# Attention kernel: second passes of the 512-wide look-ahead and score blocks as 64-row matmuls issued in a row

## The chip, the cores and the metric

The kernel runs on one core of one Trainium2 chip. The metric is the device time of one execution in microseconds. TensorE (PE) does the matmuls, ScalarE (ACT) and VectorE (DVE) read its results out of PSUM, GpSimd (POOL) masks and normalizes, and SyncE (SP) issues the DMAs.

## The reference

For each of 8 batches of 512 tokens by 256, with 8 heads of 64:

```python
xn = layernorm(x)
qu, ku, vu, qc, kc, vc = split(xn @ W_qkv.T)            # 6 x 8 heads x 64
term1 = where(causal_mask, 0.0, (qc * SCALE) @ vu.T)
lookahead = where(causal_mask, sigmoid((qu * SCALE) @ ku.T), 0.0)
Su = einsum('bhij,bhkj->bhik', term1, lookahead)
scores = (qc * SCALE) @ kc.T - silu(Su)
attn = softmax(where(causal_mask, neg, scores))
out = (attn @ vc) @ W_out.T
y = x + out + (silu(xn @ wg.T) * (xn @ wu.T)) @ wd.T
```

## The kernel before

Three stages run one after the other: a prologue that transposes `W_qkv` (to about 18 us), `attention` over all batches (to about 1000 us), and `ffn_and_sum`. The change touches `attention` alone.

Every fp32 value is kept as a high and a low part in a rounded 32-bit format, and a product is a sum of passes over them (`PRODUCTS`: high-high, high-low, low-high). Heads are 64 wide and the array has 128 rows. For the look-ahead and the scores the two halves of the rows are used: for head `h`, the 64 partitions with the head's index hold the high part of `ku` (or `kc`), the other 64 the low part; `qu_s` and `qc_s` hold for index `HIGH` the high part of q in both halves, and for `LOW` the low part in both. The first matmul of a block (`a = HIGH`) therefore sums high-high and low-high at once, the second (`a = LOW`) adds q's low part times both halves of k.

**Steps.** The stage runs 64 steps, one head each (`g = b * HEADS + s`), written out for s = 0 to 7 in a loop over batches (`FIRST` for batch 0, `MIDDLE` for 1 to 6, `LAST` for 7). Work on a head is spread over three steps: in step g the look-ahead and `term1` blocks of head g, the scores of head g - 1 (`back1`), the turning of probabilities and the product with v of head g - 2 (`back2`). Even steps also project QC, V and KC of the next pair of heads, odd steps QU, KU and VU. The order of each engine's instructions is written out by hand in `even_step` and `odd_step` of each engine, and engines are held together by counting semaphores alone; an engine's queue is in order.

**Blocks.** The causal triangle of 512 by 512 is in three groups j: j = 0 is the row block of width 512, j = 1 those of 384 and 128, j = 2 that of 256. `look_ahead(j)` (L681) is two matmuls a row block into a bank of X; ScalarE takes tanh of it (`tanh_of_L`, L875). `scores(j)` does the same products (L709) into `Sc`, then, at j = 0 after waiting for all of T and L of its head, the matmuls of `Su` (L719, twelve for j = 0) into another bank; ScalarE's `gate_of` (L899) reads `Su`, VectorE's `silu_of` (L1111) and `minus_scores` (L1122) follow.

**X banks.** Four PSUM banks are handed round in the order in which PE fills them (`X_ORDER`). A block's `into_x` waits until the block that had the bank four fills earlier has been read. For `("L", s, 0)` of an even step s = 2, 4, 6 that is the head product `("O", s - 1, 0)`, free when `sum_o` (L1154, VectorE) of the odd step is done. (In batch 0, s = 2, it is a `T` block.) For s = 0 of batches 1 to 7 it is the KU projection of step 7, and `("L", 0, 1)` has the bank of VU. In an even step `look_ahead(0)` also waits for KU's low part and for the doubled `qu_s`:

```python
if s % 2 == 0 and j == 0:
    pe.wait_ge(qu_twice, (b * PAIRS + s // 2 + 1) * 32)
    bank, filled = into_x(part, b, ("L", s, j), proj_low, lambda b: proj_count(b * PAIRS + s // 2, KU))
```

**Around the change.** PE ends an odd step with `project(KU)`, `project(VU)` (L638, six 512-wide matmuls each) and begins the even step with `scores(g - 1, s1, 0)`, then `look_ahead(0)`, `look_ahead(1)`, and the transposes of probabilities (L733). ScalarE ends the odd step with `high_proj(KU)` (L855, two copies of 64 partitions), `copy_o_low` (L921), `exp_of(2)`, `high_proj(VU)`; VectorE with `low_proj(KU)` (L1052, two), `inverse(2)`, `sum_o`, `low_proj(VU)` (L1052).

Of the kernel before, what the change touches and what calls it, by code (L numbers as in the profile page):

```python
# [11 lines left out]
P = 128  # L12
# [279 lines left out]
def attention(nc, x, w_gate, w_up, w_down, W_out, sh, heads_out):  # L292
# [4 lines left out]
    with ctx:  # L297
# [101 lines left out]
        def proj_count(q, t):  # L399

            if isinstance(q, int) and q == 0:
                return FIRST_PAIR.index(t) + 1
            return q * 5 + PROJ_ORDER.index(t) + 1
# [201 lines left out]
        def _(pe):  # L605
# [64 lines left out]
            def look_ahead(part, b, s, j):  # L670

                if s % 2 == 0 and j == 0:
                    pe.wait_ge(qu_twice, (b * PAIRS + s // 2 + 1) * 32)
                    bank, filled = into_x(part, b, ("L", s, j), proj_low,
                                          lambda b: proj_count(b * PAIRS + s // 2, KU))
                else:
                    bank, filled = into_x(part, b, ("L", s, j))
                for w in ROWS[j]:
                    J, at = w - 1, WIDE[w] - GROUP[j][0]
                    for a in (HIGH, LOW):  # L680
                        last = pe.matmul(bank[:, at:at + w * P], ku_s[:, s % 2, J * P:(J + 1) * P],  # L681
                                         qu_s[:, s % 2, a, 0:w * P], start=(a == 0), stop=(a == 1))
                last.then_inc(filled, 1)

            def term1(part, b, s, j):

                par = (s // 2) % 2
                if s % 2 == 0 and j == 0:
                    pe.wait_ge(qc_twice, (b * PAIRS + s // 2 + 1) * 32)
                    bank, filled = into_x(part, b, ("T", s, j), proj_low,  # L690
                                          lambda b: proj_count(b * PAIRS + s // 2, VU))
                else:
                    bank, filled = into_x(part, b, ("T", s, j))
                for w in ROWS[j]:
                    J, at = TT - w, WIDE[w] - GROUP[j][0]
                    for a in (HIGH, LOW):
                        last = pe.matmul(bank[:, at:at + w * P], vu_s[:, s % 2, J * P:(J + 1) * P],  # L697
                                         qc_s[:, par, s % 2, a, J * P:SEQ], start=(a == 0), stop=(a == 1))
                last.then_inc(filled, 1)

            def scores(g, s, j):

                hp, par, slot = s % 2, (s // 2) % 2, (s + j) % 2
                if not (isinstance(g, int) and 3 * g + j < 2):
                    pe.wait_ge(scores_emptied, 3 * g + j - 1)
                for w in ROWS[j]:
                    I, at = w - 1, WIDE[w] - GROUP[j][0]
                    for a in (HIGH, LOW):
                        pe.matmul(Sc[slot][:, at:at + w * P], qc_s[:, par, hp, a, I * P:(I + 1) * P],  # L709
                                  kc_s[:, par, hp, 0:w * P], start=(a == 0), stop=(a == 1))  # L710
                if j == 0:
                    pe.wait_ge(T_ready, after(g, 3, 2))
                    pe.wait_ge(L_ready, after(g, 3, 2))
                for w in ROWS[j]:
                    I, at = w - 1, WIDE[w] - GROUP[j][0]
                    for J in range(I, -1, -1):
                        to = WIDE[TT - J] + (I - J) * P
                        for n, (a, c) in enumerate(PRODUCTS):
                            last = pe.matmul(Su[slot][:, at:at + (J + 1) * P], T_s[:, hp, a, to:to + P],  # L719
                                             L_s[:, hp, c, WIDE[J + 1]:WIDE[J + 1] + (J + 1) * P],  # L720
                                             start=(J == I and n == 0), stop=(J == 0 and n == 2))
                last.then_inc(scores_filled, 1)
# [29 lines left out]

            def even_step(part, b, s, g, s1, back1, back2, ahead):
                if back1:
                    scores(g - 1, s1, 0)
                look_ahead(part, b, s, 0)
                look_ahead(part, b, s, 1)
                if back2:
                    turn_probs(part, b, s, g - 2, 0)
                    turn_probs(part, b, s, g - 2, 1)  # L760
                    turn_probs(part, b, s, g - 2, 2)
                look_ahead(part, b, s, 2)
                if back1:
                    scores(g - 1, s1, 1)
                term1(part, b, s, 0)
                if s == 6:
                    transpose_x(part, b, s, b + 1)
                if back2:
                    attend(part, b, s, g - 2)
                if back1:  # L770
                    scores(g - 1, s1, 2)
                term1(part, b, s, 1)
                term1(part, b, s, 2)
                if ahead:
                    if s == 6:
                        pe.wait_ge(xT_low, (b + 1) * KD)
                    project(part, b, s, QC, (s // 2 + 1) % PAIRS)
                    values(part, b, s)
                    project(part, b, s, KC, (s // 2 + 1) % PAIRS)
                if part == LAST:  # L780
                    turn_weights(part, b, s, WEIGHTS_IN_STEP.get(s, ()))

            def odd_step(part, b, s, g, s1, back1, back2, ahead):
                look_ahead(part, b, s, 0)
                if back1:
                    scores(g - 1, s1, 0)
                look_ahead(part, b, s, 1)
                if back2:
                    turn_probs(part, b, s, g - 2, 0)
                look_ahead(part, b, s, 2)  # L790
                if ahead:
                    project(part, b, s, QU, (s // 2 + 1) % PAIRS)
                if back2:
                    turn_probs(part, b, s, g - 2, 1)
                if back1:
                    scores(g - 1, s1, 1)
                term1(part, b, s, 0)
                if back2:
                    turn_probs(part, b, s, g - 2, 2)
                term1(part, b, s, 1)  # L800
                if back1:
                    scores(g - 1, s1, 2)
                if back2:
                    attend(part, b, s, g - 2)
                term1(part, b, s, 2)
                if ahead:
                    project(part, b, s, KU, (s // 2 + 1) % PAIRS)
                    project(part, b, s, VU, (s // 2 + 1) % PAIRS)
                if part == LAST:
                    turn_weights(part, b, s, WEIGHTS_IN_STEP.get(s, ()))  # L810
# [27 lines left out]
        def _(act):  # L838
# [83 lines left out]

            def even_step(part, b, s, g, s1, back1, back2, ahead):
                par = (s // 2 + 1) % 2
                if back1:
                    gate_of(g - 1, s1, 0)
                tanh_of_L(part, b, s, g, 0)
                tanh_of_L(part, b, s, g, 1)
                if back2:
                    high_PT(part, b, s, g - 2, 0)  # L930
                    high_PT(part, b, s, g - 2, 1)
                tanh_of_L(part, b, s, g, 2)
                if back2:
                    high_PT(part, b, s, g - 2, 2)
                high_L(g, s, 0)
                if back1:
                    gate_of(g - 1, s1, 1)
                high_T(part, b, s, g, 0)
                if s == 6:
                    high_xT(part, b, s)  # L940
                if back1:
                    exp_of(g - 1, s1, 0)
                if back2:
                    copy_o_low(part, b, s, g - 2)
                high_L(g, s, 1)
                if back1:
                    gate_of(g - 1, s1, 2)
                high_T(part, b, s, g, 1)
                high_T(part, b, s, g, 2)
                if back1:  # L950
                    exp_of(g - 1, s1, 1)
                high_L(g, s, 2)
                if ahead:
                    high_proj(part, b, s, QC, par)
                    high_values(part, b, s)
                if back1:
                    exp_of(g - 1, s1, 2)
                if ahead:
                    high_proj(part, b, s, KC, par)
                if part == LAST:  # L960
                    high_weights(part, b, s, WEIGHTS_IN_STEP.get(s, ()))
# [669 lines left out]
```

## Time and profile before

| | us |
|---|---|
| median of 2 runs | 1201.75 (1200.53 to 1202.97) |
| span of the profiled execution | 1197.5 |
| PE busy | 1155.7 |
| DVE busy | 1046.0 |
| ACT busy | 924.4 |
| POOL busy | 543.8 |

The span runs from the first to the last instruction of the profiled execution. Matmuls overlap each other, so a PE that shows as busy is not thereby at its peak: how fast blocks follow one another is read from their starts in the timeline.

### The profile page before, as it was taken

How to read it: one execution, taken by the hardware profiler on the slowest of the kernel's cores; microseconds unless marked ns; L12 is line 12 of the kernel's file. 1: busy time of each engine (PE TensorE's matmuls, PEld its weight loads, DVE VectorE, ACT ScalarE, POOL GpSimd, SP SyncE). 2: the span in 40 equal slices, each digit the busy share in tenths (PEclk: the TensorE clock that was granted, in tenths of full speed). 3: DMA queues.
4: the chain of work that ended last, by engine and by line, in shares of the span. 5: the costliest groups of instructions: out<-in, count | busy, mean ns of one | idle time of the engine just before them, and what ended most of it. 6: DMA issues, size and time to landing. Idle time of an engine off the chain costs nothing. (4 is left out here: it accounts for less than half of the span.)

```text
span 1197.5 us, 25023 instructions
## 1 busy us (share of the span) xinstructions
PE 1155.7 (97%) x7324; PEld 1049.7 (88%) x7324; DVE 1046.0 (87%) x2421; ACT 924.4 (77%) x2074; POOL 543.8 (45%) x915
## 2 busy tenths in 40 slices
PE   6999999999999999999999999999999987999997
PEld 5899898989898989898989898989899976999997
DVE  6799889989998999899989998999889987878885
ACT  5788888888888888888888888888888864434443
POOL 0455555546555555555655565556555550000000
PEclk9999999999999999999999999999999998999999
DMA  5111211121112111211121112111321112243332
GB/s 172 40 45 45 63 45 45 45 63 44 44 44 63 44 44 44 63 44 44 44 63 44 44 44 63 44 44 44 101 59 45 45 54 79 89 140 102 108 109 67
DMA packets 41491, 74.16 MB, mean 62 GB/s; under 512 B 3504, under 2 KB 24496, under 8 KB 41392
## 3 DMA queue, kind: packets, MB, share of 16 engines
q1 hardware_dynamic: 41392, 73.15, 21.2%
q14 instruction: 75, 0.61, 0.2%
q8 instruction: 24, 0.39, 0.1%
HBM read 27.00 MB, written 12.58 MB: 33 GB/s over the span
## 5 line engine op out<-in xcount | busy, mean ns | idle before, releaser
L719 PE MATMUL Su<-L_s,T_s 128*128 128x128 f32 (+3 forms) x1920 | 292.5, 299 | 1.8 <-POOL T_s L543 1.8
L719 PEld LDWEIGHTS Su<-L_s,T_s 128*128 128x128 f32 x1920 | 279.3, 190 | 16.4 <-POOL T_s L543 2.7
L553 POOL TENSOR_SCALAR prob<-prob,inv 128x512 f32<-128x512 f32 x252 | 274.5, 1096 | 13.1 <-DVE inv L1134 12.9
L638 PE MATMUL X<-xT,W 128*128 128x512 f32 x960 | 242.5, 394 | 3.0 <-PEq L130 3.0
L638 PEld LDWEIGHTS X<-xT,W 128*128 128x128 f32 x960 | 172.7, 189 | 33.6 <-issue 3.2
L527 POOL TENSOR_SCALAR_AFFINE_SELECT gate<-gate 128x128 f32<-128x128 f32 (+1 forms) x192 | 66.3, 346 | 262.3 <-DVE gate L1111 197.3
L899 ACT ACTIVATE gate<-Su 128x512 f32<-128x512 f32 (+1 forms) x192 | 101.4, 528 | 71.5 <-PE Su L719 70.4
L907 ACT ACTIVATE prob<-prob,least 128x512 f32<-128x512 f32 (+3 forms) x256 | 142.4, 561 | 7.6 <-DVE least L1122 7.2
L1111 DVE SCALAR_TENSOR_TENSOR gate<-gate,Su 128x512 f32<-128x512 f32 (+1 forms) x192 | 114.2, 595 | 27.3 <-ACT gate L899 17.4
L543 POOL TENSOR_SCALAR_AFFINE_SELECT T_s<-T_s 128x256 fp32r<-128x256 f32 x256 | 131.1, 542 | 13.3 <-DVE T_s L1103 9.2
L535 POOL TENSOR_SCALAR_AFFINE_SELECT tanh_l<-tanh_l 128x128 f32<-128x128 f32 (+1 forms) x192 | 62.6, 333 | 160.0 <-ACT tanh_l L875 157.8
L681 PE MATMUL X<-qu_s,ku_s 128*128 128x512 f32 (+3 forms) x512 | 115.2, 335 | 11.4 <-DVE vu_s L1052 6.1
L882 ACT ACTIVATE T_s<-X 128x512 fp32r<-128x512 f32 (+1 forms) x192 | 97.4, 527 | 36.7 <-PE X L697 36.7
L1141 DVE TENSOR_TENSOR PT_s<-X,PT_s 128x512 fp32r<-128x512 f32 (+1 forms) x192 | 108.8, 594 | 19.1 <-ACT PT_s L915 18.1
L1122 DVE CUSTOM_DVE_ANT_0 prob<-Sc,gate 128x512 f32<-128x512 f32 (+3 forms) x256 | 117.8, 478 | 7.5 <-issue 6.2
L1095 DVE SCALAR_TENSOR_TENSOR L_s<-tanh_l,L_s 128x512 fp32r<-128x512 f32 (+1 forms) x192 | 121.1, 631 | 1.5 <-ACT L_s L890 1.5
L697 PE MATMUL X<-qc_s,vu_s 128*128 128x512 f32 (+3 forms) x512 | 115.2, 339 | 3.3 <-DVE qu_s L1052 2.1
L1103 DVE TENSOR_TENSOR T_s<-X,T_s 128x512 fp32r<-128x512 f32 (+1 forms) x192 | 113.5, 592 | 3.7 <-ACT T_s L882 1.1
L709 PE MATMUL Sc<-kc_s,qc_s 128*128 128x512 f32 (+3 forms) x512 | 115.6, 327 | 0.2 <-DVE least L1122 0.2
L875 ACT ACTIVATE tanh_l<-X 128x512 f32<-128x512 f32 (+1 forms) x192 | 99.5, 529 | 11.5 <-PE X L681 10.5
L890 ACT ACTIVATE L_s<-tanh_l 128x512 fp32r<-128x512 f32 (+1 forms) x192 | 104.7, 564 | 2.0 <-POOL tanh_l L535 1.6
L681 PEld LDWEIGHTS X<-qu_s,ku_s 128*128 128x128 f32 x512 | 84.0, 189 | 22.8 <-DVE vu_s L1052 9.0
(85 smaller groups left out, 2132.7 us busy)
## 6 DMA issues: line engine op xcount, KB each, us to landing
qu_s<-qu_s SPq DMA_DIRECT2D x64, 256.0 KB, 3.7
qc_s<-qc_s SPq DMA_DIRECT2D x64, 256.0 KB, 3.5
xb<-in_L_attn_x SPq DMA_DIRECT2D x16, 512.0 KB, 4.6
heads_out<-o_s SPq DMA_DIRECT2D x32, 256.0 KB, 2.0
f_o_in<-heads_out SPq DMA_DIRECT2D x8, 1024.0 KB, 5.7
f_xres<-in_L_attn_x SPq DMA_DIRECT2D x8, 512.0 KB, 4.6
out<-f_y SPq DMA_DIRECT2D x8, 512.0 KB, 3.2
w_raw<-in_L_attn_W_qkv SPq DMA_DIRECT2D x6, 512.0 KB, 7.4
```

The source lines that it names most:

```text
L543: last = pool.affine_select(out=v, in_=v.bitcast(F32), compare_op=ALU.is_ge, fill=0.0, base=0, pattern=[[0, 2], [1, P]], channel_multiplie ...
L553: last = pool.tensor_scalar(v, v, inv[:, hp, w - 1:w], None, ALU.mult)
L638: last = pe.matmul(bank[:, :], sh.W[:, a, k, cols], xT[:, c, k, :], start=(n == 0), stop=(n == 3 * KD - 1))
L681: last = pe.matmul(bank[:, at:at + w * P], ku_s[:, s % 2, J * P:(J + 1) * P], qu_s[:, s % 2, a, 0:w * P], start=(a == 0), stop=(a == 1))
L697: last = pe.matmul(bank[:, at:at + w * P], vu_s[:, s % 2, J * P:(J + 1) * P], qc_s[:, par, s % 2, a, J * P:SEQ], start=(a == 0), stop=(a = ...
L709: pe.matmul(Sc[slot][:, at:at + w * P], qc_s[:, par, hp, a, I * P:(I + 1) * P], kc_s[:, par, hp, 0:w * P], start=(a == 0), stop=(a == 1))
L719: last = pe.matmul(Su[slot][:, at:at + (J + 1) * P], T_s[:, hp, a, to:to + P], L_s[:, hp, c, WIDE[J + 1]:WIDE[J + 1] + (J + 1) * P], start ...
L907: last = act.activation(v, v, ACT.Exp, bias=least[:, hp, w - 1:w], scale=-1.0, accum_out=total[:, hp, w - 1:w])
L1095: dve.scalar_tensor_tensor(L_s[:, s % 2, LOW, c:c + n], tanh_l[:, c:c + n], 1.0, L_s[:, s % 2, HIGH, c:c + n].bitcast(F32), ALU.add, ALU.s ...
L1103: dve.tensor_tensor(T_s[:, s % 2, LOW, c:c + n], bank[:, 0:n], T_s[:, s % 2, HIGH, c:c + n].bitcast(F32), ALU.subtract) \
L1111: dve.scalar_tensor_tensor(gate[:, c:c + n], gate[:, c:c + n], 1.0, Su[(s + j) % 2][:, 0:n], ALU.add, ALU.mult).then_inc(silu_done, 1)
L1122: last = dve.tensor_tensor_reduce(prob[:, hp, WIDE[w]:WIDE[w] + w * P], Sc[(s + j) % 2][:, at:at + w * P], gate[:, WIDE[w]:WIDE[w] + w * P ...
```

## The change

A new function `first_products` issues four 512-wide matmuls: the high pass of `look_ahead(0)`, the high pass of the Sc product of `scores(g - 1, s1, 0)`, and then the two second passes, each over 64 rows (the partitions that hold the high part of `ku` or `kc`; q's low part times k's low part is left out of them). As the two heads are of different parity, the two second passes lie on different halves of the array, and they go into different banks. `scores` gets an argument that leaves the products out. It is called in all 32 odd steps and in the 31 even steps with `back1`, so 63 times; in the odd steps the look-ahead was already ahead of the scores, in the even steps this order is new. In the even steps ScalarE takes `tanh_of_L(0)` ahead of `gate_of(0)`. The narrower row blocks (384, 128, 256) stay as they are, and so do the other engines and the DMAs.

```diff
--- before.py
+++ after.py
@@ -682,6 +682,27 @@
                                          qu_s[:, s % 2, a, 0:w * P], start=(a == 0), stop=(a == 1))
                 last.then_inc(filled, 1)
 
+            def first_products(part, b, s, g):
+
+                if s % 2 == 0:
+                    pe.wait_ge(qu_twice, (b * PAIRS + s // 2 + 1) * 32)
+                    bank, filled = into_x(part, b, ("L", s, 0), proj_low,
+                                          lambda b: proj_count(b * PAIRS + s // 2, KU))
+                else:
+                    bank, filled = into_x(part, b, ("L", s, 0))
+                back = g - 1
+                hp, par, slot = (s - 1) % 2, ((s - 1) % HEADS // 2) % 2, (s - 1) % 2
+                pe.matmul(bank[:, :], ku_s[:, s % 2, (TT - 1) * P:SEQ], qu_s[:, s % 2, HIGH, :], start=True, stop=False)
+                if not (isinstance(back, int) and back == 0):
+                    pe.wait_ge(scores_emptied, 3 * back - 1)
+                pe.matmul(Sc[slot][:, :], qc_s[:, par, hp, HIGH, (TT - 1) * P:SEQ], kc_s[:, par, hp, :],
+                          start=True, stop=False)
+                mine, other = slice((s % 2) * DH, (s % 2 + 1) * DH), slice(hp * DH, (hp + 1) * DH)
+                pe.matmul(bank[:, :], ku_s[mine, s % 2, (TT - 1) * P:SEQ], qu_s[mine, s % 2, LOW, :],
+                          start=False, stop=True).then_inc(filled, 1)
+                pe.matmul(Sc[slot][:, :], qc_s[other, par, hp, LOW, (TT - 1) * P:SEQ], kc_s[other, par, hp, :],
+                          start=False, stop=True)
+
             def term1(part, b, s, j):
 
                 par = (s // 2) % 2
@@ -698,12 +719,12 @@
                                          qc_s[:, par, s % 2, a, J * P:SEQ], start=(a == 0), stop=(a == 1))
                 last.then_inc(filled, 1)
 
-            def scores(g, s, j):
+            def scores(g, s, j, products_done=False):
 
                 hp, par, slot = s % 2, (s // 2) % 2, (s + j) % 2
-                if not (isinstance(g, int) and 3 * g + j < 2):
+                if not products_done and not (isinstance(g, int) and 3 * g + j < 2):
                     pe.wait_ge(scores_emptied, 3 * g + j - 1)
-                for w in ROWS[j]:
+                for w in () if products_done else ROWS[j]:
                     I, at = w - 1, WIDE[w] - GROUP[j][0]
                     for a in (HIGH, LOW):
                         pe.matmul(Sc[slot][:, at:at + w * P], qc_s[:, par, hp, a, I * P:(I + 1) * P],
@@ -752,8 +773,10 @@
 
             def even_step(part, b, s, g, s1, back1, back2, ahead):
                 if back1:
-                    scores(g - 1, s1, 0)
-                look_ahead(part, b, s, 0)
+                    first_products(part, b, s, g)
+                    scores(g - 1, s1, 0, True)
+                else:
+                    look_ahead(part, b, s, 0)
                 look_ahead(part, b, s, 1)
                 if back2:
                     turn_probs(part, b, s, g - 2, 0)
@@ -781,9 +804,8 @@
                     turn_weights(part, b, s, WEIGHTS_IN_STEP.get(s, ()))
 
             def odd_step(part, b, s, g, s1, back1, back2, ahead):
-                look_ahead(part, b, s, 0)
-                if back1:
-                    scores(g - 1, s1, 0)
+                first_products(part, b, s, g)
+                scores(g - 1, s1, 0, True)
                 look_ahead(part, b, s, 1)
                 if back2:
                     turn_probs(part, b, s, g - 2, 0)
@@ -922,9 +944,9 @@
 
             def even_step(part, b, s, g, s1, back1, back2, ahead):
                 par = (s // 2 + 1) % 2
+                tanh_of_L(part, b, s, g, 0)
                 if back1:
                     gate_of(g - 1, s1, 0)
-                tanh_of_L(part, b, s, g, 0)
                 tanh_of_L(part, b, s, g, 1)
                 if back2:
                     high_PT(part, b, s, g - 2, 0)
```

## Rows read from the trace of the kernel before

**Rows 1.** The page: busy us (share) and count of PE; granted clock in 40 slices.

```profile
PE 1155.7 (97%) x7324; PEld 1049.7 (88%) x7324; DVE 1046.0 (87%) x2421; ACT 924.4 (77%) x2074; POOL 543.8 (45%) x915
...
PEclk9999999999999999999999999999999998999999
```

**Rows 2.** Waits of PE: us in total, times, longest us.

```profile
PE X L681 <- DVE vu_s L1052: 6.1, 7, 0.9
```

**Rows 3.** Timeline, PE, 300 to 334 us: start, us, instructions, [idle before <-releaser].

```profile
316.14 2.92 PE L638 MATMUL X<-xT,W 128*128 128x512 f32 x12
318.90 0.62 PE L709 MATMUL Sc<-kc_s,qc_s 128*128 128x512 f32 x2
319.35 2.02 PE L719 MATMUL Su<-L_s,T_s 128*128 128x512 f32 x12
321.50 1.25 PE L681 MATMUL X<-qu_s,ku_s 128*128 128x512 f32 x6
322.59 1.28 PE L733 MATMUL X<-ident,prob 128*128 128x128 f32 x10
323.62 0.48 PE L681 MATMUL X<-qu_s,ku_s 128*128 128x256 f32 x2
```

**Rows 4.** Timeline, all engines, the same stretch.

```profile
317.73 1.20 ACT L855 ACTIVATE ku_s<-X 64x512 fp32r<-64x512 f32 x2
...
318.96 1.39 DVE L1052 TENSOR_TENSOR ku_s<-X,ku_s 64x512 fp32r<-64x512 f32 x2 [0.20 <-ACT ku_s L855]
...
320.58 0.69 DVE L1154 TENSOR_TENSOR o_s<-X,o_low 64x512 f32<-64x512 f32 x1
...
321.29 1.39 DVE L1052 TENSOR_TENSOR vu_s<-X,vu_s 64x512 fp32r<-64x512 f32 x2
```

**Rows 5.** Timeline, PE, the same place in batches 0 and 7.

```profile
79.27 0.62 PE L709 MATMUL Sc<-kc_s,qc_s 128*128 128x512 f32 x2
...
81.74 1.25 PE L681 MATMUL X<-qu_s,ku_s 128*128 128x512 f32 x6
...
918.16 0.62 PE L709 MATMUL Sc<-kc_s,qc_s 128*128 128x512 f32 x2
...
920.63 1.23 PE L681 MATMUL X<-qu_s,ku_s 128*128 128x512 f32 x6
```

**Rows 6.** Timeline, the same place at s = 0, batch 1: DVE, then PE.

```profile
138.57 1.39 DVE L1052 TENSOR_TENSOR ku_s<-X,ku_s 64x512 fp32r<-64x512 f32 x2 [0.20 <-ACT ku_s L855]
...
138.50 0.62 PE L709 MATMUL Sc<-kc_s,qc_s 128*128 128x512 f32 x2
...
140.81 0.67 PE L681 MATMUL X<-qu_s,ku_s 128*128 128x512 f32 x2
142.35 0.78 PE L681 MATMUL X<-qu_s,ku_s 128*128 128x384 f32 x4 [0.87 <-DVE vu_s L1052]
```

**Rows 7.** Groups of PE by shape, 200 to 900 us: busy us, mean ns.

```profile
L709 PE MATMUL Sc<-kc_s,qc_s 128*128 128x512 f32 x92 | 28.6, 392 | 0.0
```

**Rows 8.** Timeline, PE, 957 to 972 us; then that stretch by windows (PE, PEld, DVE, ACT, POOL, PEclk).

```profile
964.14 0.73 PE L681 MATMUL X<-qu_s,ku_s 128*128 128x512 f32 x2 [2.35 <-DVE W L1075]
...
965.17 3.57 PE L719 MATMUL Su<-L_s,T_s 128*128 128x512 f32 x12
968.58 0.74 PE L681 MATMUL X<-qu_s,ku_s 128*128 128x384 f32 x4
...
965.16:968.56 3.40, 3.40 (x13) 3.10 (x12) 1.94 (x2) 0.34 (x1) 0.46 (x2) 0.50 0.59 188
```

**Rows 9.** Timeline, PE, two other long waits; then windows behind them.

```profile
17.84 6.40 PE L638 MATMUL X<-xT,W 128*128 128x512 f32 x27 [2.97 <-PEq L130]
...
993.35 2.40 PE L733 MATMUL X<-ident,prob 128*128 128x128 f32 x10 [3.23 <-DVE prob L1256]
...
19.67:23.07 3.40, 3.40 (x17) 2.81 (x16) 2.28 (x4) 3.02 (x6) 0.00 (x0) 1.00 0.00 0
992.47:999.28 6.81, 5.93 (x25) 5.72 (x26) 6.31 (x12) 4.25 (x10) 0.00 (x0) 0.50 0.01 2
```

## Prediction

> **What bounds the kernel now.** I read first the page's busy shares [rows 1]: TensorE is busy in 97% of the span, and the granted clock is full nearly everywhere. Then the PE timeline of one odd and one even head step in the middle of the attention stage [rows 3]: the blocks follow one another with no idle in brackets, so in this stage the bound is the stream of matmuls, and a 512-wide one costs its pitch, (318.90 - 316.14) / 12 = 0.230 us, although each lasts 0.392 [rows 7]. A saved pass is worth 0.23 us, and any wait of PE is paid in full. What PE waits for, little as it is, stands at one place: the look-ahead at the head of an even step [rows 2]. So the third view is what the other engines do there [rows 4]. The reader is to see a chain that starts only when the KU projection (the first six of the twelve matmuls from 316.14) has been written: ScalarE copies its high part from 317.73, VectorE subtracts to 318.96 + 1.39 = 320.35, then comes `sum_o` from 320.58 to 321.27, and the look-ahead matmul starts at 321.50. That is 0.23 us behind `sum_o`, which frees the PSUM bank that `look_ahead(0)` writes. The whole of `scores(g - 1, s1, 0)`, from 318.90 on, lies in front of it and hides the chain. The cover is nearly used up: in a step without this release the two Sc matmuls and the twelve Su matmuls take 140.81 - 138.50 = 2.31 us [rows 6], here 321.50 - 318.90 = 2.60, so PE already waits 0.29.
>
> **Part 1, the even steps: the look-ahead goes ahead of the scores.** `first_products` begins with the waits of `look_ahead(0)` (`qu_twice`, the bank, `proj_low` of KU), and everything else of PE is queued behind them: the Sc products and the Su matmuls too, whose inputs are ready. Nothing on ScalarE or VectorE starts the chain earlier, as its head is a PE matmul and each link runs as soon as the one before it ends [rows 4]. So the look-ahead starts when it starts now, and PE stands from 318.90 to 321.50, 2.60 us. (In batches 0 and 7 it is 81.74 - 79.27 = 2.47 us, and the same at 918.16 [rows 5]; the release there is 0.13 us quicker.)
>
> What that costs is counted at the next block, `look_ahead(1)`. Before, it follows 0.46 us after L0. After, there lie between them two high passes (0.46), the pair of second passes (p), and the Su matmuls, 2.31 - 0.46 = 1.85 us. The loss is 1.85 + p a step. There are 31 even steps with `back1`. In the seven at s = 0 of batches 1 to 7 the bank comes from KU's projection and not from O, so the release is KU's low part, done at 138.57 + 1.39 = 139.96 [rows 6]; with the 0.23 us that the release takes elsewhere PE starts at 140.19 rather than 138.50. There the present wait of 0.87 us for the bank of VU, in front of `look_ahead(1)` (7 such waits [rows 2]), disappears behind the Su matmuls: `look_ahead(1)` comes at 140.19 + 0.46 + p + 1.85 against 142.35, a loss of 0.15 + p. The other 24 lose 1.85 + p.
>
> **Part 2, the pair, p.** Two 512-wide passes of 128 rows become two of 64 rows on different halves, into different banks. No row of the trace has a 64-row matmul, so p is bounded: below by one pass, 0.23, if both stream at once; above by two in a row, 0.46, with the array emptied on both sides as the next bound. What lies between is the second matmul's own weight load. The nearest row is the transposes, one load and one 128-wide matmul each, at a pitch of (323.62 - 322.59) / 10 = 0.103 us [rows 3]. I take p = 0.23 + 0.11 = 0.34: the second starts one load later and overlaps the rest. In the 32 odd steps the look-ahead was ahead of the scores already, so four passes (0.92) become 0.46 + p = 0.80: a gain of 0.12 us each.
>
> For this pair the Trainium skill (TensorE: Matmul & The Clock Gate, Part 3 on packing small matmuls) says that matmuls on different row groups run side by side in about the time of one; p would be 0.23 by it and the result some 7 us lower. No row here shows it.
>
> **Part 3, the moved ScalarE instruction.** In the even steps `tanh_of_L(0)` now goes ahead of `gate_of(0)`. Its input comes before Su's by the Su block, 1.85 us, and it takes about 0.6, so it is over before the gate could start: nothing, and covered by those Su matmuls. VectorE and POOL orders are unchanged; their work in the step (gate, silu, PT, masks) hangs on PE blocks that all shift together. The `scores_emptied` wait is for a group emptied a step earlier. No DMA moves, and the SP queue is passed by nothing.
>
> **Part 4, the clock.** A stall of 2.6 us is long enough to ask about the granted clock. Row by row [rows 8]: PE waited 2.35 us before 964.14, and from 965.16 the clock was 0.50 (1.2 GHz) for 3.4 us; the twelve Su matmuls from 965.17 to 968.58 took 3.41 us where they take 1.85, a loss of 1.56. After the 3.23 us before 993.35 the clock stood at 0.50 [rows 9], but after the 2.97 us before 17.84 it was still 1.00, and after the seven waits of 0.87 it stayed full. So a stall of this length brings the clock down often, not always. I take 14 of the 24 long stalls, each at 1.56 us: 21.8 us. The seven of 1.69 us I take as harmless.
>
> **The sum.** 24 x (1.85 + 0.34) = 52.6; 7 x (0.15 + 0.34) = 3.4; 32 x -0.12 = -3.8; clock 21.8. Together +74.0 us. The profiled span of 1197.5 becomes 1271.5; the runs' median of 1201.75 stands 4.25 above that span, so the time is 1275.8, say 1276 us, 6.2% slower.
>
> **The rivals.**
> - *The stall without the clock.* As above, but the clock stays full. For it: 17.84 and the short waits. 52.2 us more, 1254 us; with p = 0.23 it is 24 x 2.08 + 7 x 0.38 - 32 x 0.23 = 45.2, 1247.
> - *The clock falls at every long stall.* 24 x 1.56 = 37.4 in place of 21.8: 1292 us. For it: two of the three long waits read.
> - *The array is emptied around each pair.* A matmul's end trails its pitch by 0.392 - 0.230 = 0.16 us [rows 3, 7]; if the full-height work must drain before the half-height pair and the pair before the Su matmuls, p = 0.23 + 0.32 = 0.55, and 63 x 0.21 = 13 us come on top: 1289; with the clock falling each time, 1305. The Trainium skill (TensorEngine Tiling (Array Packing), Key Properties) speaks for this one: a change of tiling mode drains the engine. No run here shows it.
> - *The chain is ready in time* (the other side). The step would gain if the bank and KU's low part were released by 318.90. Then PE never stands: 63 x 0.23 = 14.5 from pairs that overlap fully and 18 x 0.29 = 5.2 from the present waits, 1182 us. It decides at 318.90; `sum_o` ends 2.37 us later, and its head is the PE matmul itself, so I see nothing that could bring it forward.
>
> **How the numbers follow.** The forecast with part of the clock falls 0.50; clock never 0.19; clock always 0.17; drain 0.10; chain ready in time 0.04. The range runs from the stall with full overlap and full clock, 1247, to just short of the drain with all the clock falls, 1302. The likeliest case's own range is 1262 to 1288 (8 to 20 falls, p from 0.23 to 0.46). A difference under 2% (24 us) is about what a measurement of this kernel can't tell from none. All cases but the last are slower by more than that, 0.96; the last lies within 2%, 0.03, and I leave 0.01 for faster.
>
> **What would show it.** Right: in the profile after, about 24 idle gaps of PE in front of the look-ahead of even steps, 2.4 to 2.6 us each and put down to VectorE, seven of about 1.7, none in odd steps; the waits of 0.87 gone; granted-clock digits in the attention slices lowered to 8 or so. The pair: the start of the Su matmuls 0.80 us behind the start of the look-ahead. Wrong: if look-ahead and Sc products of even steps start directly behind the VU projection, the wait was misread; if Su starts under 0.7 or over 0.9 us behind, p was; if the clock in the attention slices stays full, the clock term falls away and leaves 1254.

## The result and the profile after

The changed kernel takes 1305.57 us (median of 2 runs, 1305.31 to 1305.84) against 1201.75: a ratio of 1.0868, 95% interval 1.0836 to 1.0900. The forecast was 1276, range 1247 to 1302. The direction and the place were right, the size was 30 us short, and the time lies 3.6 us outside the range.

| | before | after |
|---|---|---|
| median of the runs, us | 1201.75 | 1305.57 |
| span of the profiled execution, us | 1197.5 | 1304.0 |
| PE busy, us | 1155.7 | 1205.1 |
| DVE busy, us | 1046.0 | 1047.3 |

The page of the kernel after has the granted clock in 40 slices (compare [rows 1]):

```profile
PEclk9999999999999999999999999999999989999999
```

The slices are too coarse to show short stretches of a lower clock: the row reads 9 almost everywhere, as before. The mean clock of the span says more. It was 0.991 before and is 0.961 now:

```profile
core 0: 1304.0 us, clock 0.961
```

The waits of PE, in total, times, longest, in place of the one line of [rows 2]:

```profile
PE X L695 <- DVE o_s L1176: 55.7, 23, 2.5
PE X L695 <- DVE ku_s L1074: 12.4, 8, 2.8
```

31 waits in front of the look-ahead of the 31 even steps, where there were 7 of 0.87 us in front of its second block; the two lines share them by which of VectorE's results came last. In the odd steps there is none but the 2.35 us in the last of them, which the kernel before has too [rows 8]. The timeline of PE at one such step (the place of [rows 3], step g = 20) and at g = 50:

```profile
346.90 2.91 PE L638 MATMUL X<-xT,W 128*128 128x512 f32 x12
352.26 0.49 PE L695 MATMUL X<-qu_s,ku_s 128*128 128x512 f32 x1 [2.45 <-DVE o_s L1176]
352.59 0.40 PE L698 MATMUL Sc<-kc_s,qc_s 128*128 128x512 f32 x1
352.92 0.62 PE L701 MATMUL X<-qu_s,ku_s 64*128 64x512 f32 x1
352.92 0.61 PE L703 MATMUL Sc<-kc_s,qc_s 64*128 64x512 f32 x1
353.47 3.52 PE L740 MATMUL Su<-L_s,T_s 128*128 128x512 f32 x12
356.82 0.73 PE L681 MATMUL X<-qu_s,ku_s 128*128 128x384 f32 x4
...
852.48 0.49 PE L695 MATMUL X<-qu_s,ku_s 128*128 128x512 f32 x1 [2.45 <-DVE o_s L1176]
...
853.57 2.15 PE L740 MATMUL Su<-L_s,T_s 128*128 128x512 f32 x12
855.55 0.63 PE L681 MATMUL X<-qu_s,ku_s 128*128 128x384 f32 x3
```

The twelve projection matmuls start at 346.90 and need 12 x 0.230 = 2.76 us, so PE is free at 349.66 and starts again at 352.26: 2.60 us. The first fragment then shows the Su matmuls from 353.47 to 356.82, 3.35 us, and a clock of 0.50 in this stretch (columns: PE, PEld, DVE, ACT, POOL busy, then PEclk):

```profile
353.20:356.50 3.30, 3.30 (x11) 2.75 (x10) 0.24 (x1) 0.60 (x1) 0.00 (x0) 0.50 0.20 73
```

At g = 50 the stall is the same and the clock stayed full: Su takes 1.98 us. The chain that PE waits for, on VectorE (KU's low part, then `sum_o`):

```profile
349.72 1.39 DVE L1074 TENSOR_TENSOR ku_s<-X,ku_s 64x512 fp32r<-64x512 f32 x2 [0.20 <-ACT ku_s L877]
...
351.33 0.69 DVE L1176 TENSOR_TENSOR o_s<-X,o_low 64x512 f32<-64x512 f32 x1
```

`sum_o` ends at 352.02 and PE starts 0.24 us later, as in [rows 4]. At s = 0 (here g = 16) PE waits for KU's low part only (compare [rows 6]):

```profile
285.97 0.50 PE L695 MATMUL X<-qu_s,ku_s 128*128 128x512 f32 x1 [1.36 <-DVE ku_s L1074]
...
289.03 0.74 PE L681 MATMUL X<-qu_s,ku_s 128*128 128x384 f32 x4
```

An odd step, where nothing waits:

```profile
334.34 0.39 PE L695 MATMUL X<-qu_s,ku_s 128*128 128x512 f32 x1
334.57 0.39 PE L698 MATMUL Sc<-kc_s,qc_s 128*128 128x512 f32 x1
334.89 0.50 PE L701 MATMUL X<-qu_s,ku_s 64*128 64x512 f32 x1
334.89 0.50 PE L703 MATMUL Sc<-kc_s,qc_s 64*128 64x512 f32 x1
335.32 2.14 PE L740 MATMUL Su<-L_s,T_s 128*128 128x512 f32 x12
337.29 0.74 PE L681 MATMUL X<-qu_s,ku_s 128*128 128x384 f32 x4
```

The two 64-row matmuls start together at 334.89, but 0.32 us behind the matmul before them, and Su starts 0.43 us behind them.

### The profile page after: what moved, and what is told of

The parts are those of the page before. It is cut to its first block and busy times, and to the rows that moved or that the text cites. A ratio compares the mean times of both kernels' runs of the same rounds, so it can differ in the third digit from the quotient of the medians.

```text
span 1304.0 us, 25023 instructions
## 1 busy us (share of the span) xinstructions
PE 1205.1 (92%) x7324; PEld 1061.2 (81%) x7324; DVE 1047.3 (80%) x2421; ACT 924.4 (71%) x2074; POOL 541.4 (42%) x915
## 5 line engine op out<-in xcount | busy, mean ns | idle before, releaser
L740 PE MATMUL Su<-L_s,T_s 128*128 128x128 f32 (+3 forms) x1920 | 330.8, 323 | 1.1 <-POOL T_s L543 1.1
L740 PEld LDWEIGHTS Su<-L_s,T_s 128*128 128x128 f32 x1920 | 302.2, 206 | 31.0 <-issue 17.4
L543 POOL TENSOR_SCALAR_AFFINE_SELECT T_s<-T_s 128x256 fp32r<-128x256 f32 x256 | 128.1, 529 | 13.8 <-DVE T_s L1125 9.7
L937 ACT ACTIVATE PT_s<-X 128x512 fp32r<-128x512 f32 (+1 forms) x192 | 98.2, 531 | 1.4 <-PE X L754 0.7
L754 PE MATMUL X<-ident,prob 128*128 128x128 f32 x640 | 92.7, 275 | 4.2 <-DVE prob L1278 3.2
L695 PE MATMUL X<-qu_s,ku_s 128*128 128x512 f32 x63 | 27.9, 442 | 70.4 <-DVE o_s L1176 55.7
```

Of the source, the lines that this page charges most:

```text
L543: last = pool.affine_select(out=v, in_=v.bitcast(F32), compare_op=ALU.is_ge, fill=0.0, base=0, pattern=[[0, 2], [1, P]], channel_multiplie ...
```

## The experiments

**The order alone, and the pairs in odd steps alone.** First the changed kernel's order with 128-row second passes:

```diff
-pe.matmul(bank[:, :], ku_s[mine, s % 2, (TT - 1) * P:SEQ], qu_s[mine, s % 2, LOW, :],
+pe.matmul(bank[:, :], ku_s[:, s % 2, (TT - 1) * P:SEQ], qu_s[:, s % 2, LOW, :],
...
-pe.matmul(Sc[slot][:, :], qc_s[other, par, hp, LOW, (TT - 1) * P:SEQ], kc_s[other, par, hp, :],
+pe.matmul(Sc[slot][:, :], qc_s[:, par, hp, LOW, (TT - 1) * P:SEQ], kc_s[:, par, hp, :],
```

> The changed kernel with its order (look-ahead ahead of the scores in even steps, tanh ahead of the gate, two high passes and then two second passes) but with the second passes over all 128 rows as before. Theory (the wait of the order and the clock falls behind it cost most, the 64-row pairs a small part): PE still stands 2.6 us before the look-ahead of 24 even steps and 1.5 at the seven s = 0; 24 x (2.61 + 0.92 + 1.87 - 3.06) = 56, 7 x 0.45 = 3, the clock falls 24 times at 1.5 = 36: 1201.75 + 95 = about 1297 us, with four 512-wide starts 0.23 apart. Rival (the 64-row pairs are the cause, by draining the array): near 1202 us.

It took 1288.01 us (one run; the kernel before 1200.70 on the same chip). Its timeline of PE, an odd step and then an even one:

```profile
329.55 0.39 PE L695 MATMUL X<-qu_s,ku_s 128*128 128x512 f32 x1
329.77 0.39 PE L698 MATMUL Sc<-kc_s,qc_s 128*128 128x512 f32 x1
330.00 0.39 PE L701 MATMUL X<-qu_s,ku_s 128*128 128x512 f32 x1
330.23 0.40 PE L703 MATMUL Sc<-kc_s,qc_s 128*128 128x512 f32 x1
330.47 2.03 PE L740 MATMUL Su<-L_s,T_s 128*128 128x512 f32 x12
332.33 0.56 PE L681 MATMUL X<-qu_s,ku_s 128*128 128x384 f32 x2
...
380.78 0.49 PE L695 MATMUL X<-qu_s,ku_s 128*128 128x512 f32 x1 [2.48 <-DVE o_s L1176]
...
383.64 0.56 PE L681 MATMUL X<-qu_s,ku_s 128*128 128x384 f32 x2
```

Four starts 0.23 apart, and 332.33 - 329.55 = 2.78 us from the look-ahead to its second block; in the kernel after it is 337.29 - 334.34 = 2.95. In the even step, at full clock, it is 383.64 - 380.78 = 2.86, against 855.55 - 852.48 = 3.07. So the order alone brings 87 of the 104 us, without one 64-row matmul. The expectation of 1297 was 9 us high: I had taken 24 falls of the clock and there were 18, which at 1.5 us each is the 9 us.

Then the pairs with the even steps as before:

```diff
 def even_step(part, b, s, g, s1, back1, back2, ahead):
     if back1:
-        first_products(part, b, s, g)
-        scores(g - 1, s1, 0, True)
-    else:
-        look_ahead(part, b, s, 0)
+        scores(g - 1, s1, 0)
+    look_ahead(part, b, s, 0)
```

(and ScalarE's order of the even step as before).

> The 64-row pairs in the 32 odd steps only; even steps in PE's and ScalarE's order of the kernel before. Theory (a pair costs more than two full passes, since the array is emptied around it): from the start of the look-ahead to the block behind Su 2.96 us in place of 2.79, 32 x 0.17 = 5.4: about 1207 us. Rival (the halves overlap and save a pass; all of the loss is the order): 32 x -0.12 or better, 1198 us or less. No change of the clock by either.

1204.99 us (median of 6), ratio 1.0041 (1.0028 to 1.0053): the pairs lose time where no wait is near. Its odd steps show the starts of the kernel after, 0, 0.23, 0.55, 0.55, 0.98. The control has the same order with 128-row passes:

> As the kernel with pairs in odd steps only, but the second passes over 128 rows: only the order of the four 512-wide matmuls in odd steps differs from the kernel before (high, high, low, low). Theory: nothing of the loss comes from this order, 1202 us within 2. Rival (alternating banks and weights slows the stream): as slow as with the pairs, about 1207.

1201.70 us (median of 10), ratio 1.0008 (0.9998 to 1.0018). The order of the four matmuls is free; the loss of about 3.3 us between the two (5.4 by the 0.17 us a step that the traces show; the other parts of the steps got some 2 us shorter) is the 64 rows'.

**The clock.** Matmuls that do nothing useful fill most of the stall:

```diff
 if s % 2 == 0:
+    if not (isinstance(back, int) and back == 0):
+        pe.wait_ge(scores_emptied, 3 * back - 1)
+    for i in range(6 if s == 0 else 10):
+        pe.matmul(Sc[slot][:, :], qc_s[:, par, hp, HIGH, (TT - 1) * P:SEQ], kc_s[:, par, hp, :],
+                  start=True, stop=True)
     pe.wait_ge(qu_twice, (b * PAIRS + s // 2 + 1) * 32)
...
```

> The changed kernel with ten 512-wide matmuls (six at s = 0) more into the Sc bank at the head of every even step, before the waits; the true product overwrites them. They run while PE would stand, 10 x 0.23 = 2.3 of the 2.6 us. Theory (each long stall brings the granted clock to 0.5 for one stretch, 24 x 1.5 us = 36): the clock stays full in the attention stage and the time falls to 1305.6 - 36 = about 1270 us although PE has 292 matmuls more to do. Rival (the clock has little to do with it, the time is the wait's alone): 1305 us or more.

(The count is 24 x 10 + 7 x 6 = 282, not 292.) It took 1277.98 us (one run): 27.6 us less with 282 matmuls more. The timeline of PE in one even step, and the mean clock, which is back near the 0.991 of before:

```profile
341.67 2.45 PE L693 MATMUL Sc<-kc_s,qc_s 128*128 128x512 f32 x10
344.27 0.49 PE L702 MATMUL X<-qu_s,ku_s 128*128 128x512 f32 x1
...
345.36 2.12 PE L747 MATMUL Su<-L_s,T_s 128*128 128x512 f32 x12
347.32 0.74 PE L681 MATMUL X<-qu_s,ku_s 128*128 128x384 f32 x4
...
core 0: 1276.3 us, clock 0.989
```

Su takes 1.96 to 1.98 us in all 31 even steps, so no stall is followed by the lower clock any more. The rest is as it was: the look-ahead starts 344.27 - 341.67 = 2.60 us behind the end of the projections, and its second block 3.05 behind it. The gain is 27.6 and not 36 us because of the seven steps with s = 0, which take 1.1 us longer than in the kernel after, 8 us together: in five of them the fillers began 1.3 to 1.9 us late, put down to issue, and pushed the look-ahead back. The five are those of batches 2 to 6, where PE comes back to the start of the loop; in batches 1 and 7 they began on time. Why the return costs this here is open: in the kernel before the Sc matmuls at the same place start on time in all seven.

**What the pair costs, and where.** Three kernels, pairs in odd steps only, one run each; to be compared with the 1204.99 of one pair. First both 64-row matmuls on the same half, so that the scores lose q's low times k's high part and get low times low:

```diff
-mine, other = slice((s % 2) * DH, (s % 2 + 1) * DH), slice(hp * DH, (hp + 1) * DH)
+mine = other = slice((s % 2) * DH, (s % 2 + 1) * DH)
```

> Pairs in odd steps only, but both 64-row second passes lie on the same 64 rows of the array (the scores' second pass then multiplies q's low part with k's low part; low times high is left out). Theory (the two halves do stream at once, what costs is around the pair): the second matmul starts 0.23 us or more behind the first, and the front from the look-ahead to Su grows from 0.98 to 1.2 us; 32 x 0.23 = 7 us over the kernel with pairs in odd steps, about 1212. Rival (the pair doesn't overlap, the equal start times are only how the records show it): front 0.98, time 1205.

1212.95 us, 8.0 more (7 expected). The second passes and the first of Su on PE:

```profile
338.75 0.49 PE L701 MATMUL X<-qu_s,ku_s 64*128 64x512 f32 x1
339.09 0.39 PE L703 MATMUL Sc<-kc_s,qc_s 64*128 64x512 f32 x1
339.41 2.15 PE L740 MATMUL Su<-L_s,T_s 128*128 128x512 f32 x12
```

On one half they start 0.34 us apart, on two halves together; the front to Su is 1.20 for 0.98. So the overlap is real. The Trainium skill (TensorE: Matmul & The Clock Gate, Part 3) says that matmuls on different row tiles run side by side. The trace agrees: the two starts are within 0.01 us on two halves and 0.34 apart on one.

Second, each 64-row matmul straight behind its own 128-row one, four changes of height for two:

```diff
 pe.matmul(bank[:, :], ..., qu_s[:, s % 2, HIGH, :], start=True, stop=False)
+pe.matmul(bank[:, :], ku_s[mine, ...], qu_s[mine, s % 2, LOW, :], start=False, stop=True).then_inc(filled, 1)
...
 pe.matmul(Sc[slot][:, :], qc_s[:, par, hp, HIGH, ...], kc_s[:, par, hp, :], start=True, stop=False)
-pe.matmul(bank[:, :], ku_s[mine, ...], qu_s[mine, s % 2, LOW, :], start=False, stop=True).then_inc(filled, 1)
 pe.matmul(Sc[slot][:, :], qc_s[other, par, hp, LOW, ...], kc_s[other, par, hp, :], start=False, stop=True)
```

> Pairs' matmuls in odd steps only, each 64-row matmul straight behind its own 128-row one: high, low, high, low, so four changes of the array's height in place of two, and no overlap. Theory (a change of height costs, 0.17 for the two around a pair above two full passes, or 0.29 + 0.11 above one pass): a matmul ahead of a change 0.32, a 64-row one ahead of a change back 0.43, front 2 x (0.32 + 0.43) = 1.50 us; 32 x (1.50 - 0.98) = 17 us over the kernel with pairs in odd steps, about 1222. Rival (a 64-row matmul is itself slow, whatever stands beside it): four of 0.23 to 0.3, front near 1.0 to 1.1, about 1208.

1218.56 us, 13.6 more (17 expected). PE in an odd step:

```profile
337.80 0.40 PE L696 MATMUL X<-qu_s,ku_s 128*128 128x512 f32 x1
338.13 0.50 PE L697 MATMUL X<-qu_s,ku_s 64*128 64x512 f32 x1
338.56 0.49 PE L701 MATMUL Sc<-kc_s,qc_s 128*128 128x512 f32 x1
338.99 0.50 PE L703 MATMUL Sc<-kc_s,qc_s 64*128 64x512 f32 x1
339.42 2.12 PE L740 MATMUL Su<-L_s,T_s 128*128 128x512 f32 x12
```

Starts at 0.33, 0.76, 1.19, and Su at 1.62 where 1.50 was expected: every matmul with a change of height behind it takes 0.33 to 0.43 until the next start, where the pitch is 0.23. The Trainium skill (TensorEngine Tiling (Array Packing), Key Properties) says that a change of mode drains the engine. The trace agrees that a change costs time, 0.10 to 0.20 us each; that the array is empty at that moment it can't show, as the ends of matmuls are modelled. The time grew by less than the front (32 x 0.64 = 20 us): read over all steps, the stretches from the projections to the second look-ahead block in odd steps grew by 19.4 us and the other parts of the steps got 4.6 us shorter, most of it where the `term1` matmuls follow the transposes.

Third, the pair twice in a row (the second passes are summed twice):

> Pairs in odd steps only, each pair issued twice in a row (the second passes are summed twice), so four 64-row matmuls of 512 columns between the same two changes of height. Theory (edges cost once, a pair streams in the time of one pass): front 0.98 + 0.23 = 1.21 us, 32 x 0.23 = 7 us over the kernel with one pair, about 1212; a further pair would then be cheaper than the two full passes (0.46) it stands for. Rival (every 64-row matmul pays): front 1.4 us or more, 1219 or more.

1210.81 us, 5.8 more (7 expected). PE in an odd step:

```profile
338.29 0.39 PE L695 MATMUL X<-qu_s,ku_s 128*128 128x512 f32 x1
...
338.84 0.49 PE L701 MATMUL X<-qu_s,ku_s 64*128 64x512 f32 x1
...
339.17 0.39 PE L705 MATMUL X<-qu_s,ku_s 64*128 64x512 f32 x1
...
339.50 2.12 PE L744 MATMUL Su<-L_s,T_s 128*128 128x512 f32 x12
341.46 0.74 PE L681 MATMUL X<-qu_s,ku_s 128*128 128x384 f32 x4
```

From the look-ahead to its second block 341.46 - 338.29 = 3.17 us, 0.22 more than with one pair. So a further pair costs one pass of 0.23 and the changes are paid once. With 128-row passes the same work would take 2.78 + 0.46 = 3.24, an estimate. One pair loses 0.17 us, two in a row would win 0.07 by it. (This kernel has no second 512-wide pair ready at that point.)

**The chain behind the stall.** The changed kernel, with `copy_o_low` ahead of `exp_of(1)` on ScalarE (behind `high_proj(VU)` at s = 7) and, on VectorE:

```diff
+if back2 and s != 7:
+    sum_o(part, b, s, g - 2)
 if ahead:
     low_proj(part, b, s, KU, par, q)
 if back1:
     inverse(g - 1, s1, 2)
-if back2:
-    sum_o(part, b, s, g - 2)
 if ahead:
     low_proj(part, b, s, VU, par, q)
+if back2 and s == 7:
+    sum_o(part, b, s, g - 2)
```

> The changed kernel, with the O bank's release taken out of the chain at the end of odd steps: copy_o_low on ScalarE ahead of exp(1), sum_o on VectorE ahead of low_proj(KU), except at s = 7. Theory (PE's stall before the look-ahead of the 24 even steps is the length of the chain behind the KU projection): the stall ends 0.23 us behind KU's low part instead of sum_o; ScalarE's KU copy may come up to 0.5 later for the copy put ahead, so the stall falls from 2.6 to 1.7 to 2.2 us, and the clock falls at fewer of them: 24 x 0.4 to 0.9 = 10 to 22 us and up to 36 more, 1250 to 1296. Rival (the stall is that of the 64-row matmul's change of array or of code loading): unchanged, 1305.

1300.17 us (one run), 5.4 less. The waits of PE, and VectorE's `sum_o` and KU part:

```profile
PE X L695 <- DVE ku_s L1076: 65.2, 31, 2.8
...
349.57 0.68 DVE L1178 TENSOR_TENSOR o_s<-X,o_low 64x512 f32<-64x512 f32 x1
350.18 1.38 DVE L1076 TENSOR_TENSOR ku_s<-X,ku_s 64x512 fp32r<-64x512 f32 x2
```

All 31 waits are now for KU's low part, so the chain was named rightly. But it isn't shorter. `sum_o` stands ahead of KU on VectorE, and ScalarE's copy of O delays its KU copy: KU's low part is done at 351.56, 2.36 us behind the end of the projections (346.44 + 2.76 = 349.20), where in the changed kernel `sum_o` was done 352.02 - 349.66 = 2.36 behind it. What shrank is the time from VectorE's last result to the look-ahead, 0.06 us here for 0.24 behind `sum_o`. So the stall is 2.41 to 2.43 us for 2.60 in 18 steps, in five of the six in batches 0 and 7 it grew by 0.06, and over all 31 even steps it is 2.8 us less. The clock fell behind 20 of the stalls, once for twice as long, where there were 24 falls; the stretch from the projections to the second look-ahead block in the even steps is 8.5 us shorter in all, so that 5.7 us are the falls'. The mean clock hides this, 0.962 for 0.961, as other stretches of the span had more of the lower clock. The expectation was too high by half at least: it had KU's low part up to 0.5 us later, and it came 0.9 later.

**The same chain in the kernel before.** The waits of 0.29 and 0.87 us that the kernel before has at this place [rows 3, 6] should yield too. `sum_o` now goes ahead of `inverse(1)`, where VectorE has room, and at s = 7 both O instructions go behind the VU parts (the lines that these replace are left out):

```diff
# ScalarE
 high_T(part, b, s, g, 2)
+if back2 and s != 7:
+    copy_o_low(part, b, s, g - 2)
 exp_of(g - 1, s1, 1)
...
 high_proj(part, b, s, VU, par)
+if back2 and s == 7:
+    copy_o_low(part, b, s, g - 2)
# VectorE
 low_L(g, s, 1)
+if back2 and s != 7:
+    sum_o(part, b, s, g - 2)
 inverse(g - 1, s1, 1)
...
 low_proj(part, b, s, VU, par, q)
+if back2 and s == 7:
+    sum_o(part, b, s, g - 2)
```

> The kernel before, its PE order and 128-row passes untouched, with the two releases that PE waits for brought forward. At s = 1, 3, 5: copy_o_low on ScalarE ahead of exp(1), sum_o on VectorE ahead of inverse(1), so that the look-ahead of the next even step waits for KU's low part only. At s = 7: copy_o_low and sum_o behind the VU projection's parts, so that the bank of VU comes free earlier. Theory (the same chain that became 2.6 us of stall costs the kernel before 0.29 us in 18 steps and 0.87 in 7): the two waits go, 18 x 0.29 + 7 x 0.87 = 11 us less, about 1190; at least half of it. Rival (ScalarE and VectorE are as full as PE, and what is put ahead delays the KU chain by as much): 1198 to 1203.

1196.16 us (median of 5; the kernel before 1201.24 on the same chip), ratio 0.9961 (0.9947 to 0.9975): both kernels beaten, if by little. PE at an even step and at s = 0:

```profile
318.01 0.62 PE L709 MATMUL Sc<-kc_s,qc_s 128*128 128x512 f32 x2
...
320.33 0.85 PE L681 MATMUL X<-qu_s,ku_s 128*128 128x512 f32 x3
...
321.43 1.40 PE L733 MATMUL X<-ident,prob 128*128 128x128 f32 x10
322.59 0.48 PE L681 MATMUL X<-qu_s,ku_s 128*128 128x256 f32 x2
...
380.66 0.61 PE L681 MATMUL X<-qu_s,ku_s 128*128 128x384 f32 x2 [0.38 <-DVE vu_s L1054]
```

From Sc to the look-ahead 320.33 - 318.01 = 2.32 for 2.60, and 0.38 us of wait for 0.87. That makes 18 x 0.28 + 7 x 0.49 = 8.5 us by the trace; the medians give 5.1, a little under the half that was expected at least. The trace shows where the rest went: summed over all steps, the stretch from the projections to the second look-ahead block in the even steps got 9.7 us shorter and the rest of the steps 4.6 longer, nearly all of it at the next block of the even steps, the transposes of probabilities, which took 322.59 - 321.43 = 1.16 us for 323.62 - 322.59 = 1.03 [rows 3] and began a little later behind the look-ahead. What PE waits for there was not tried. The s = 7 part alone:

> As the kernel with both releases brought forward, but with the s = 7 part alone: copy_o_low and sum_o behind the VU projection's parts, the other odd steps as in the kernel before. Theory: the seven waits of 0.87 us ahead of the second look-ahead block go, 6 us less, about 1195. Rival: the wait moves to the bank of O, which the first block of turned probabilities takes next, and little is won: 1199 to 1201.

1198.37 us (median of 11), ratio 0.9977 (0.9967 to 0.9986): 2.9 us of 6, about the 7 x 0.49 = 3.4 that the wait shrank by.

## Why the prediction was right or wrong

**Right: the wait.** The look-ahead starts when it started before, and PE stands for the 2.60 us read off before. At s = 0 it stands 1.51 us (predicted 1.69), of which the row shows 1.36 as idle, behind the modelled end of the last projection; the difference is the release, 0.05 us behind KU's low part, where the prediction carried over the 0.23 from `sum_o`. ScalarE's exchange was not run alone; with it and 128-row passes the parts of all steps behind the second look-ahead block take 724.5 us for 724.0, so it cost nothing that shows. No wait arose in the odd steps.

**Wrong: p, the term for the pair.** The step that failed is p = 0.34 for a pair. The Su matmuls start 0.98 us behind the look-ahead, beyond the 0.9 that the prediction named as its sign of being wrong. Predicted from the look-ahead to its second block 0.80 + 1.85 = 2.65 us; measured 2.95 in odd steps and 3.07 in even ones at full clock. I had priced the second matmul's weight load (0.11), but the two start together and that costs nothing; the two changes of height cost 0.39 (2.95 less 0.46 + 0.23 + 1.87). The mechanism stood among the rivals at 0.10, with p = 0.55; counted as in the prediction the measured p is 2.95 - 0.46 - 1.85 = 0.64. A further 0.1 us in the even steps is no property of the pair: the kernel with 128-row passes has it too (2.86 for 2.78), the first matmul behind a stall takes 0.33 until the next. Nor is it new: the kernel before has it behind its wait of 0.29 us. Its second look-ahead block at the place of [rows 3]:

```profile
322.07 0.51 PE L681 MATMUL X<-qu_s,ku_s 128*128 128x384 f32 x2
```

That is 0.57 us behind the first, 321.50, and not the 0.46 of the prediction, so from Sc to it were 3.17 us and not 3.06: here the prediction was 0.11 us a step too high, and in the sum the slower first matmul falls out. The odd steps' gain of 0.12 was a loss of 0.16 (2.95 for 2.79).

**Wrong: the number of clock falls.** The mechanism was right; the term that was too small is the count of 14, and 24 were measured. I took 14, from a stall of 2.35 that was followed by the lower clock and one of 2.97 that was not. Read step by step, 22 of the 24 long stalls were, and 2 of the 7 short ones. The mean clock agrees: 1304.0 x 0.039 less 1197.5 x 0.009 is 40 us of missing clock, and 24 stretches like that of [rows 8], 3.4 us at 0.50, are 41. The sign that was named for it, digits of 8 in the row of slices, did not appear: 24 falls in the 1015 us of the stage leave a mean of 0.96. The price was right: 4.56 us against 3.07 from the look-ahead to its second block, 1.49 (1.56 predicted). What sets the stalls without a fall apart is open: gaps of 2.2 to 2.8 us were followed by a fall in 22 of 24 cases here, in 18 of 24 with 128-row passes and in 19 of 24 in the kernel with the O parts brought forward.

**The sum with the measured terms.**

| term | predicted | measured |
|---|---|---|
| 24 long stalls | 24 x 2.19 = 52.6 | 24 x (2.60 + 3.07 - 3.17) = 60.0 |
| 7 at s = 0 | 3.4 | 7 x (1.51 + 3.06 - 3.85) = 5.0 |
| 32 odd steps | -3.8 | 32 x 0.16 = 5.1 |
| clock | 14 x 1.56 = 21.8 | 24 x 1.49 = 35.8 |
| sum | 74.0 | 105.9 |

(3.17 and 3.85 are the times from Sc to the second look-ahead block before; the 3.06 at s = 0 is 289.03 - 285.97.) The spans differ by 106.5. The table takes one step of each kind for all. Summed over every step, the stretch from the projections to the second look-ahead block grew by 98.4 us in the even steps (the table has 100.8; behind the 24 falls it is 1.40 us longer on average and not 1.49), by 5.1 in the odd ones, and the rest of the span by 3.0. Of the 31.9 us between the two sums of the table 17.9 lie in the three rows with p and 14.0 in the number of falls.

Two of my rivals, the pair that costs more than two full passes and the clock falling at each stall, were both near the truth; together they stood in the text as 1305, and the range ended 3 us below, since I held the two for unlikely in company. That 1305 fits to 1 us is in part luck: it has 37.4 us of clock for the 34 measured, and 0.55 for the p of 0.64. (Two figures in the prediction are off by its own sum: the rival with all falls comes to 1291, and 8 to 20 falls with p from 0.23 to 0.46 give 1259 to 1293.)

The experiments divide the 104 us: about 87 for the order (1288.01), of which 18 x 1.49 = 27 are the clock's; the rest, 17, came with the 64 rows: 63 x 0.17 = 11 for the changes of height, and the remaining 6 or so go with the falls of the clock, 24 for 18. That difference is one of two counts in single profiles and not a shown effect of the 64 rows: 1288.01 is one run too.

## What to carry to other kernels

Before a block is moved ahead of another on a full engine, ask what the other one hid: here 2.3 us of Su and Sc matmuls covered a chain of projection, copy, subtraction and bank release, and the saving of a pass of 0.23 us was paid for with 2.6. A stall of 2.2 to 2.8 us in a stream of matmuls is best priced with a lower clock behind it: 59 of 72 had one in the three kernels that stall so, at about 1.5 us each, and 3 of 21 stalls of 1.4 us. Half-height pairs do run at once, but entering and leaving the mode costs more than one saved pass, so put two or more pairs in a row or leave it. An instruction moved ahead on a full engine delays what it passes: look where the chain ends on every engine, and at the next block too.

## What was not expected of the hardware

The two 64-row matmuls on different halves start within 0.01 us of each other, weight loads included. A change between 128 and 64 rows costs 0.39 us for both ways together, around a pair of 512-wide matmuls. A gap of 2.3 to 2.8 us was followed by a granted clock of 0.50 (1.2 GHz) in 22 of 24 cases, and filling the gap with matmuls whose result is thrown away made the kernel 28 us faster. PE started 0.24 us behind `sum_o` but 0.05 behind KU's low part.
